# Summing the softmax denominators of two key blocks on VectorE before one TensorE product, in five groups of the last attention

## The reference, cut to what matters

```python
def _causal_attn(q, k, v, mask):
    scores = jnp.einsum('bhqd,bhkd->bhqk', q, k) * scale
    scores = jnp.where(mask, scores, -jnp.inf)
    attn = jax.nn.softmax(scores, axis=-1)
    return jnp.einsum('bhqk,bhkd->bhqd', attn, v)
...
y1 = _causal_attn(q1, k1, v, mask)
y2 = _causal_attn(q2, k2, v, mask)
y = y1 - lambda_full * y2
```

## Time and profile before

| what | value |
|---|---|
| median of three runs | 840.95 us (840.45 to 841.15) |
| the profiled execution: its own time / its span | 839.71 us / 837.9 us |
| the attention loop in it | 747.9 us (first scores) to 804.9 us (first product of the down projection) |
| granted TensorE clock over the loop | 1.00 |
| one cycle of three units | about 6.6 us |

### The profile page before, as it was taken

The page is one execution under the profiler, slowest core; times in us unless marked ns, Lnnn a source line. Parts: engine busy times, 40 slices in busy tenths (PEclk is TensorE's granted clock), DMA queues, the critical chain, the costliest instruction groups (busy, mean ns, idle before and its releaser), DMA issues.

```text
span 837.9 us, 15615 instructions
## 1 busy us (share of the span) xinstructions
PE 826.0 (99%) x5436; PEld 709.6 (85%) x5436; DVE 624.9 (75%) x1267; ACT 478.4 (57%) x953; POOL 471.2 (56%) x327
## 2 busy tenths in 40 slices
PE   8999999999999999999999999999999999999998
PEld 7888888888867899999999888888889988876688
DVE  6899999999997665665567788687676785436767
ACT  3666666666674565655553475743453435367743
POOL 6676767677684855575757021019948316718820
PEclk9999999999999999999999999999999999999999
DMA  8101010000005385556313150011111010030001
GB/s 340 43 20 38 19 38 19 28 28 19 19 1 188 146 283 184 184 166 193 110 32 94 59 201 14 1 52 51 38 38 38 14 63 1 1 151 4 2 2 51
DMA packets 23345, 62.19 MB, mean 74 GB/s; under 512 B 3137, under 2 KB 13633, under 8 KB 20225
## 3 DMA queue, kind: packets, MB, share of 16 engines
q1 hardware_dynamic: 21760, 57.35, 19.8%
q0 software_dynamic: 1536, 4.20, 1.6%
HBM read 50.00 MB, written 8.39 MB: 70 GB/s over the span
## 4 chain that ended last, share of the span: by engine, by line
PE 88%; DVE 6%; POOL 2%; ACT 2%; issue 1%; DMA 1%; SPq 0%; DVEq 0%; POOLq 0%
PE banks L102 26%; PE banks L104 26%; PE banks L103 26%; PE banks L1387 3%; POOL arenaC L875 1%; PE banks L1373 1%; PE banks L1023 1%; PE banks L967 1%; PE banks L966 1%; DVE x L1457 1%; DVE arenaB L1892 1%; PE banks L888 1%; PE banks L1010 1%; PE banks L1056 1%; DMA arenaC<-in_wqkv 1%
## 5 line engine op out<-in xcount | busy, mean ns | idle before, releaser
L2153 ACT ACTIVATE banks<-banks,small 128x512 f32<-128x512 f32 x128 | 84.9, 664 | 70.8 <-DVE small L1522 70.8
L1522 DVE TENSOR_REDUCE small<-banks 128x1 f32<-128x512 f32 x128 | 86.7, 677 | 4.4 <-PE banks L104 4.4
L104 PE MATMUL banks<-arenaC_rounded,arenaD_rounded 128*128 128x512 f32 (+1 forms) x256 | 89.4, 349 | 0.0
L102 PE MATMUL banks<-xnT_rounded,arenaD_rounded 128*128 128x512 f32 x224 | 87.8, 392 | 1.1 <-POOL arenaC_rounded L741 0.9
L103 PE MATMUL banks<-s_tok_rounded,arenaD_rounded 128*128 128x512 f32 x224 | 87.2, 389 | 0.0
L104 PE MATMUL banks<-xnT_rounded,arenaD_rounded 128*128 128x512 f32 x192 | 74.8, 390 | 0.0
L104 PE MATMUL banks<-xnT_rounded,arenaC_rounded 128*128 128x512 f32 x192 | 74.7, 389 | 0.0
L102 PE MATMUL banks<-arenaC_rounded 128*128 128x512 f32 (+1 forms) x192 | 70.9, 369 | 1.2 <-DVE arenaC L1537 0.6
L1537 DVE SCALAR_TENSOR_TENSOR arenaC<-banks,small,arenaC 128x512 f32<-128x512 f32 x96 | 71.2, 741 | 0.0
L103 PE MATMUL banks<-arenaD_rounded,arenaC_rounded 128*128 128x512 f32 (+1 forms) x192 | 67.9, 354 | 0.0
L727 POOL TENSOR_TENSOR arenaD_rounded<-arenaC,ones 128x512 fp32r<-128x512 f32 x30 | 31.3, 1042 | 47.4 <-DVE arenaC L1537 46.5
(11 more groups left out here) (445 smaller groups left out, 2689.3 us busy)
## 6 DMA issues: line engine op xcount, KB each, us to landing
arenaD<-in_wexp SPq DMA_DIRECT2D x8, 1060.0 KB, 5.8
arenaD<-in_wexp SPq DMA_DIRECT2D x8, 1024.0 KB
arenaC<-in_wqkv SPq DMA_DIRECT2D x16, 384.0 KB, 3.0
arenaD<-in_wexp SPq DMA_DIRECT2D x8, 512.0 KB, 3.6
slots<-arenaB SPq DMA_DIRECT2D x1, 2560.0 KB, 9.9
arenaB<-in_sw SPq DMA_DIRECT2D x1, 2084.0 KB, 7.5
arenaC<-in_wo SPq DMA_DIRECT2D x1, 2048.0 KB, 15.3
arenaC<-slots SPq DMA_DIRECT2D x8, 256.0 KB, 3.2
```

Source lines behind the costliest of these rows:

```text
L102: pe.matmul(o, r(lhs[0]), r(rhs[0]), start=start, stop=False)
L104: return pe.matmul(o, r(lhs[1]), r(rhs[0]), start=False, stop=stop)
L1522: dve.tensor_reduce(negmax[:, n % 4:n % 4 + 1], bank[3 + n % 4][:, :], AX.X, ALU.max, negate=True).then_inc(max_done, 1)
L2153: act.activation(prob[r], prob[r], ACT.Exp, bias=negmax[:, r:r + 1], accum_out=rowsum[:, r:r + 1]).then_inc(exp_done, 1)
```

## The change

In the groups 3, 5, 11, 13 and 15 (g = 1, 2, 5, 6, 7), VectorE adds the exponentials of the two key blocks of the unit off the diagonal into a new tile `zsum` (128 x 4 heads x 256, float32), which lies where `klo3[0]` was (so VectorE waits once, before its loop, until the transfers out of that region have landed). In program order the add stands directly before `normalise` of the group, so behind `normalise` of the group before. TensorE takes the products with v as before, then waits for the add and makes four products with ones (one a head) in place of eight. g = 3 and 4 are left as they were.

```diff
+        SUMMED3 = [UNITS3.index((g, 1, 0)) for g in (1, 2, 5, 6, 7)]
+        zsum = part(arenaC, 10240, 1024, r="p (h n) -> p h n", h=4)
...
+        zsum_done, ZSUM0 = ctxT_split, NT // 2
...
                     mix3(m, u, 0)
-                    mm = mix3(m, u, 1)
+                    if u in SUMMED3:
+                        pe.wait_ge(zsum_done, ZSUM0 + SUMMED3.index(u) + 1)
+                        for hh in range(4):
+                            mm = pe.matmul(bank[6 + m % 2][32 * hh:32 * hh + 32, 256:512], ones[:, 0:32], zsum[:, hh, :],
+                                           start=False, stop=True, tile_position=(0, 32 * hh))
+                    else:
+                        mm = mix3(m, u, 1)
                     if u == GROUPS3[m][-1]:
                         mm.then_inc(av_ready, 1)
...
+                def summed(u):
+
+                    dve.wait_ge(exp3_done, 2 * u + 2)
+                    dve.tensor_tensor(zsum, prob3[u % 4][:, :, 0:256], prob3[u % 4][:, :, 256:512], ALU.add).then_inc(zsum_done, 1)
+
+                dve.wait_ge(stack_in[0], 16 * STACK_PARTS[0])
                 for m in range(len(MIXES3)):
+                    u = GROUPS3[m][-1]
+                    if u in SUMMED3:
+                        summed(u)
                     normalise(m)
```

## The result

| | before | after |
|---|---|---|
| median | 840.82 us (20 runs) | 842.06 us (20 runs, 841.47 to 842.86) |
| ratio to before, 95% interval | | 1.0015 (1.0008 to 1.0021) |
| span of the profiled execution | 837.9 us | 839.9 us |
| first scores, start | 747.91 | 749.00 |
| first product of the down projection, start | 804.88 | 806.86 |

What follows compares the result with a forecast made beforehand. TensorE was taken to lead, with GpSimd and VectorE close behind. The terms from group 9 on summed to +1.16 us, taking the profiled 839.71 to 840.87 and the median to 842.1 us, range 840.5 to 843.5.

Steps and rivals of the forecast that it cites:

- Saving 0.43 us a unit: On TensorE, four products with ones fewer at each of five units save 0.43 us each, 2.15 us at most.
- The add: On VectorE, each of five adds of 128 x 1024 float32 in SBUF takes 1.23 us with no mask in the way.
- The ring: Add, products with ones, two normalise steps, next add: 6.52 us a cycle against 6.72 and 6.65 now.
- The waking of TensorE: Time from the end of a VectorE operation to the TensorE product it releases: 0.15 us.
- The masks' hold: GpSimd masks in SBUF lengthen the adds of units 17 and 20 by 0.32 us; masks behind come 0.98 us later.
- The last group: Unit 23: add done at 805.35, products with ones at 805.50, down projection at 806.04 instead of 804.88.
- the last group alone loses: Only the loop's last group loses what the others could gain, as nothing follows to keep TensorE busy: +1.16 us.
- Groups 3 and 5 at nothing: These early groups were costed at zero, as TensorE's mask waits behind them absorb shifts; at most 0.43 us kept each.
- TensorE's waits: TensorE was to wait for VectorE about 0.5 us at units 17 and 20 and 0.8 at unit 23.
- TensorE never stands longer than about half a microsecond: Claim about TensorE's idle stretches, from which four products instead of eight were said to change no clock.
- The sum: Tally from group 9 to the down projection: +1.16 us, spread about half a microsecond, chance 0.62.
- held in full: Rival: adds of units 17 and 20 meet masks just begun, pushed masks hold TensorE: +2.76 us, 843.7, chance 0.24.

Runs made afterwards that it cites:

- without7: The change at g = 1, 2, 5 and 6 only, the last group as in the kernel before: 840.75 us against 839.50 before.
- early5: The changed kernel with its five adds one place earlier in VectorE's order, before the diagonal group's division: 838.92 us against 840.58 for the kernel before.

## Why the prediction was right, point by point

- **Saving 0.43 us a unit.** Right: five of them gave 1.96 us by themselves, and putting them back behind the wait cost 2.18.
- **The add.** 1.23 us was taken, 1.22 measured where no mask ran. Reading two halves of each row cost nothing extra here.
- **The ring.** 6.52 us was the sum, 6.43 the bare ring. The waking of TensorE was too long a term: the add of unit 17 ends at 791.43 + 1.57 = 793.00 and the products start at 793.06, 0.06 and not 0.15 us. The other terms held (2.32, 2.13, and 793.76 - 793.06 = 0.70 for 0.69).
- **The masks' hold.** 0.32 longer was forecast for units 17 and 20; 1.57 and 1.58 less 1.22 is 0.35. The push of 0.98 us was right.
- **The last group.** From the reciprocal of group 13 to the down projection 6.37 us were forecast and 6.30 measured; the difference is chiefly the waking term (0.05 in place of 0.15). But "the last group alone loses" was wrong as a statement of cause. The pushed mask of unit 22 stood in the sum, hidden behind the last add; without7 shows that it loses 0.70 us by itself. The sum took the later of the two and so came out right; its own line, unit 22 at 802.5 in place of 801.72, already said that the other groups lose.
- **Groups 3 and 5 at nothing.** The reciprocal of group 9 stands 785.99 - 747.91 = 38.08 us after the first scores before and 786.98 - 749.00 = 37.98 after: 0.10 us kept.
- **TensorE's waits.** About 0.5 us was forecast at units 17 and 20, and 0.22 came at unit 20: the pushed mask of unit 19 held TensorE before it reached the add, so part of the wait moved there. In sum the same. At unit 23 0.8 was forecast and 0.60 came. There the mask of unit 22 was in the sum; it is VectorE that came earlier, its add ending 57.24 us after the first scores where 805.35 - 747.91 = 57.44 was forecast, and the waking that was shorter. The prediction's "TensorE never stands longer than about half a microsecond" contradicts its own 0.8 and was too low (0.86 us idle before unit 22); the clock stayed at 1.00 all the same.
- **The sum.** +1.16 forecast, +0.89 in the loop, 1.24 between the medians. The loop is 0.27 us shorter than forecast: 0.10 was kept ahead of group 9, 0.10 is the two cycles behind it (13.58 us for 13.68) and 0.07 the last group. In the last two, a waking term 0.09 or 0.10 us too long, three times, is set against holds 0.02 to 0.03 too short, twice. That the median met the forecast within 0.1 us is in part luck: the loop was 0.27 us better than the sum, and about 0.34 us came from outside the span, where the prediction had nothing and which no run explains.
- The rival "held in full" named the right mechanism, and the Trainium skill's rule in "SBUF — State Buffer", section "SBUF: two separate sides", holds here: in the changed kernel no add took over 1.58 us, as each of the first four met a mask in its second half, and the masks behind waited for the whole add. The price of that rival, +2.76 us, did not come, as no add met a mask at its start. early5 shows the other side of the rule: an add placed between masks takes 1.23.

## What to carry to other kernels

An engine that is idle a third of the cycle (here 2.1 to 2.2 of 6.7 us) may still have no time *at the place* where the new work stands: before moving work to it, close the ring of waits (producer, consumer, what the consumer releases) and compare its sum with the present cycle. Here the same five adds cost 0.9 us of loop in one place of VectorE's order and gained 1.8 us one place earlier (1.2 and 1.7 between the medians), where their inputs come just in time and their reader is still busy. At the end of a loop the last instance counts in full, since nothing covers it (0.8 us here). Where two engines hold each other up in SBUF, as the adds and the masks do here, the order decides how often they meet. And an effect of a thousandth is better read from the length of a stretch that the edit can reach than from the total alone, which here moved by another third of a microsecond outside the span.

## What was not expected

The early place was meant to take the add out of TensorE's way. That it would also miss the masks was not foreseen: it waits 0.48 us for ScalarE's exponentials in four of five units, which is just when GpSimd has nothing to do. In early5 the four adds of units 8, 17, 20 and 23 take 1.22 to 1.23 us, and only that of unit 5 meets a mask (1.57 us).
